# Windowed attention with q and k handled together: fewer, wider VectorE and GpSimd instructions, and alternating values matmuls

## The reference, cut to what matters

```python
h = shift_token(x)
q, k, v = jnp.split(h @ wqkv, 3, axis=-1)          # to 8 heads of 64
q = l2norm(q) * qs
k = l2norm(k) * ksc
q, k = rotary_xpos(q, k)                           # q*cos*scale + rotate_half(q)*sin*scale, k likewise with 1/scale
...
sim = jnp.einsum('bhwid,bhwjd->bhwij', bq * 8.0, look_around(bk))   # windows of 64, own and previous
attn = jax.nn.softmax(where(mask, -max, sim), axis=-1)
out = jnp.einsum('bhwij,bhwjd->bhwid', attn, look_around(bv))
x = x + out @ wo
...
x = x + (a * gelu(g)) @ w2 + b2                    # a, g from a layer norm and w1
```

## Time and profile before

| what | value |
|---|---|
| median of 3 runs | 2024.12 us (2023.77 to 2026.48) |
| the profiled execution, its own time | 2023.84 us |
| its span in the trace | 2022.0 us |
| PE, PEld busy | 1660.5 us (82%), 1363.3 us (67%) |
| DVE, ACT, POOL busy | 1419.8 us (70%), 1157.7 us (57%), 1091.1 us (54%) |
| mean granted TensorE clock | 0.937 |

### The profile page before, as it was taken

One profiled execution on the slowest core, in us unless ns is written; L12 is line 12 of the kernel. 1 busy time (PEld: TensorE's weight loads), 2 busy tenths in 40 slices (PEclk: granted clock), 3 DMA queues, 4 the chain that ended last, 5 costly groups with the idle time before them and its releaser, 6 DMA issues.

```text
span 2022.0 us, 48409 instructions
## 1 busy us (share of the span) xinstructions
PE 1660.5 (82%) x15864; PEld 1363.3 (67%) x15864; DVE 1419.8 (70%) x3769; ACT 1157.7 (57%) x3315; POOL 1091.1 (54%) x1090
## 2 busy tenths in 40 slices
PE   1898989888989899746756749989897889898984
PEld 1677878776878777525535537777776777777773
DVE  6686868676868687455655648868786768786873
ACT  1676757565757576412312227767675767576671
POOL 2774848464848485221231247757565657566650
PEclk9999999999999999978968979999998999999997
DMA  7231212122212121031010032111122221112113
GB/s 255 66 98 40 47 40 60 47 78 63 47 39 53 39 48 38 12 128 42 0 41 21 0 83 47 44 46 42 49 49 84 50 61 44 49 38 51 36 37 107
DMA packets 183672, 112.13 MB, mean 55 GB/s; under 512 B 86721, under 2 KB 164129, under 8 KB 182945
## 3 DMA queue, kind: packets, MB, share of 16 engines
q1 hardware_dynamic: 183456, 109.12, 20.4%
HBM read 43.41 MB, written 23.42 MB: 33 GB/s over the span
## 4 chain that ended last, share of the span: by engine, by line
PE 68%; DVE 11%; issue 6%; ACT 5%; SPq 3%; DMA 3%; POOL 2%; DVEq 0%; POOLq 0%; ACTq 0%
PE QK L345 12%; PE OB L690 10%; PE TT L578 7%; PE SC L619 6%; PE QK L578 5%; PE OB L645 5%; PE VB L345 4%; DVE o_n L977 4%; PE OB L578 4%; PE TT L345 3%; PE SC L601 2%; ACT probs L1098 2%; PE OB L745 2%; PE VB L745 2%; PE SC L782 2%
## 5 line engine op out<-in xcount | busy, mean ns | idle before, releaser
L1098 ACT ACTIVATE probs<-SC,shift,qgain 128x128 f32<-128x128 f32 x1024 | 457.4, 469 | 96.8 <-DVE shift L896 96.6
L1222 POOL TENSOR_TENSOR ve<-mv,epsilon 128x1 f32<-128x1 f32 x128 | 24.3, 190 | 529.1 <-DVE mv L940 529.1
L345 PE MATMUL QK<-w_qkv,hT 128*128 128x512 f32 x768 | 226.8, 433 | 19.9 <-DMA w_qkv<-qkv_d 10.5
L1098 ACT ACTIVATION_READ_ACCUMULATOR probs<-SC,shift,qgain 128x1 f32 x1024 | 220.0, 215 | 0.0
L1235 POOL TENSOR_TENSOR rnorm<-clip,mhalf 128x8 f32<-128x8 f32 x128 | 211.2, 1650 | 15.0 <-DVE clip L905 14.9
L578 PE MATMUL TT<-ident,probs 128*128 128x128 f32 x1280 | 194.4, 280 | 25.0 <-ACT probs L1098 18.4
L888 DVE TENSOR_REDUCE top<-SC 128x4 f32<-128x512 f32 x256 | 175.4, 685 | 56.0 <-PE SC L619 56.0
L1244 POOL TENSOR_TENSOR qgain<-clip,mhalf 128x8 f32<-128x8 f32 x128 | 209.4, 1636 | 0.0
L578 PEld LDWEIGHTS TT<-ident,probs 128*128 128x128 f32 x1280 | 156.9, 144 | 64.7 <-issue 20.8
L949 DVE TENSOR_TENSOR rope_c<-QK,rope 128x512 f32<-128x512 f32 x256 | 172.9, 676 | 35.9 <-PE QK L345 34.8
L954 DVE TENSOR_TENSOR rope_s<-QK,rope 128x256 f32<-128x256 f32 x512 | 190.3, 412 | 0.0
(11 more groups left out here) (136 smaller groups left out, 3908.6 us busy)
## 6 DMA issues: line engine op xcount, KB each, us to landing
v_prev<-v_own SPq DMA_DIRECT2D x256, 128.0 KB, 2.3
x_att<-stream SPq DMA_DIRECT2D x128, 64.0 KB, 2.1
h<-stream SPq DMA_DIRECT2D x256, 32.0 KB, 1.8
stream<-x_new SPq DMA_DIRECT2D x32, 256.0 KB
w_qkv<-qkv_d SPq DMA_DIRECT2D x3, 1536.0 KB, 6.6
h<-x_mid SPq DMA_DIRECT2D x128, 32.0 KB
h<-x_mid SPq DMA_DIRECT2D x128, 31.8 KB
rope<-rope_d SPq DMA_DIRECT2D x24, 128.0 KB, 3.2
```

The costliest lines, as they stand in the source:

```text
L345: last = mm(dst, fr(left(a)), fr(right(b)), start=(k == 0), stop=(k == 2))
L1098: last = nc.scalar.activation(probs[:, b, hd, :], SC[:, hd * P:hd * P + P], ACT.Exp, bias=shift[:, b, hd:hd + 1], scale=qgain[:, b, hd % 4 ...
```

## The change

DVE's rotation takes q and k in one instruction for the cosines and two for the sines, where there were two and four, and waits once, for both products. The maximum is one instruction over 8 heads and the shift one over 8 heads; both stand ahead of `o_n`. The clip is one instruction. The factor 8 on q, which was in the clip of q, is put into q's tables on the host. POOL adds q and k in one instruction into the new buffer `qk_r`, and scales the keys in it in place. ACT's first exponential waits for the single shift. The values product goes head by head, first and second window in turn.

```diff
-        q_r = sb("q_r", [P, 2, INNER])
-        k_a = sb("k_a", [P, INNER])
-        k_r = sb("k_r", [P, 2, INNER])
+        qk_r = sb("qk_r", [P, 2, 2 * INNER])
...
-                        for m, signal in ((0, s_q), (1, s_k)):
-                            product(mm, QK[:, m * 512:m * 512 + 512], lambda x: hT[:, b, x, :],
-                                    lambda x: w_qkv[:, x, m * 512:m * 512 + 512]).then_inc(signal, 1)
+                        for m in range(2):
+                            last = product(mm, QK[:, m * 512:m * 512 + 512], lambda x: hT[:, b, x, :],
+                                           lambda x: w_qkv[:, x, m * 512:m * 512 + 512])
+                        last.then_inc(s_k, 1)
...
-                        for w, v in ((0, v_prev), (1, v_own)):
-                            for hd in range(HEADS):
+                        for hd in range(HEADS):
+                            for w, v in ((0, v_prev), (1, v_own)):
...
-            def highest(t, half):
+            def highest(t):
 
                 dve.wait_ge(s_s, t.count())
-                v.tensor_reduce(top[:, t.i % 2, 4 * half:4 * half + 4],
-                                SC[:, half * 512:half * 512 + 512].rearrange("q (h k) -> q h k", h=4),
+                v.tensor_reduce(top[:, t.i % 2, :], SC[:, :].rearrange("q (h k) -> q h k", h=HEADS),
                                 AX, ALU.max).then_inc(s_mx, 1)
...
-                v.tensor_scalar(clip2[:, b, 8:16], norm2[:, b, 8:16], 1e-24, None, ALU.max).then_inc(s_cl, 1)
                 need(dve, s_qg, t.count(back=2))
-                v.tensor_scalar(clip2[:, b, 0:8], norm2[:, b, 0:8], 1e-24, QK_SCALE ** -2,
-                                ALU.max, ALU.mult).then_inc(s_cl, 1)
+                v.tensor_scalar(clip2[:, b, :], norm2[:, b, :], 1e-24, None, ALU.max).then_inc(s_cl, 1)
...
-                    need(dve, s_ka, t.count(back=1))
-                    for m, signal in ((0, s_q), (1, s_k)):
-                        dve.wait_ge(signal, t.count())
-                        src = qk(QK[:, :])[:, m]
-                        v.tensor_tensor(qk(rope_c[:])[:, m], src,
-                                        rope[:, i, m, 0:1, :].to_broadcast([P, HEADS, DH]), ALU.mult)
-                        sin = rope[:, i, m, 1:2, :]
-                        for half in range(2):
-                            a, o = 32 * half, 32 * (1 - half)
-                            last = v.tensor_tensor(qk(rope_s[:])[:, m, :, a:a + 32], src[:, :, o:o + 32],
-                                                   sin[:, :, a:a + 32].to_broadcast([P, HEADS, 32]), ALU.mult)
+                    dve.wait_ge(s_k, t.count())
+                    v.tensor_tensor(qk(rope_c[:]), qk(QK[:, :]),
+                                    rope[:, i, :, 0, :].unsqueeze(2).to_broadcast([P, 2, HEADS, DH]), ALU.mult)
+                    for half in range(2):
+                        a, o = 32 * half, 32 * (1 - half)
+                        last = v.tensor_tensor(qk(rope_s[:])[:, :, :, a:a + 32], qk(QK[:, :])[:, :, :, o:o + 32],
+                                               rope[:, i, :, 1, a:a + 32].unsqueeze(2).to_broadcast([P, 2, HEADS, 32]),
+                                               ALU.mult)
...
-                act.wait_ge(s_sh, t.count(unit=2) + (half - 1))
+                act.wait_ge(s_sh, t.count())
...
-                    g.tensor_tensor(q_r[:, b, :], rope_c[:, 0:512], rope_s[:, 0:512], ALU.add).then_inc(s_qr, 1)
-                    need(pool, s_kr, t.count(back=1))
-                    g.tensor_tensor(k_a[:], rope_c[:, 512:1024], rope_s[:, 512:1024], ALU.add).then_inc(s_ka, 1)
+                    g.tensor_tensor(qk_r[:, b, :], rope_c[:], rope_s[:], ALU.add).then_inc(s_qr, 1)
```

More of the change, by code:

```diff
@@ L164, in build @@
         clip2 = sb("clip2", [P, 2, 2 * HEADS])
-        rnorm = sb("rnorm", [P, 2, HEADS])
-        qgain = sb("qgain", [P, 2, HEADS])
+        rnorm = sb("rnorm", [P, 2, 2, HEADS])
         rope_c = sb("rope_c", [P, 2 * INNER])
         rope_s = sb("rope_s", [P, 2 * INNER])
-        q_r = sb("q_r", [P, 2, INNER])
-        k_a = sb("k_a", [P, INNER])
-        k_r = sb("k_r", [P, 2, INNER])
+        qk_r = sb("qk_r", [P, 2, 2 * INNER])
         qT = sb("qT", [P, 2, PAIRS, P])
@@ L333, in build @@
         w1_of = [(w_1[:, 0, :], w_1[:, 1, :]),
-                 tuple(buf[:].rearrange("p b n -> p (b n)")[:, 0:2 * HID] for buf in (q_r, k_r))]
-        y_T = q_r[:].rearrange("p b n -> p (b n)")
+                 tuple(qk_r[:, b, 0:2 * HID] for b in range(2))]
+        y_T = qk_r[:, 0, :]
         def fr(ap):
@@ L631, in f @@
                             pe.wait_ge(s_sq, t2.count())
-                        for m, src in ((1, k_r), (0, q_r)):
+                        for m in (1, 0):
                             for c in range(PAIRS):
-                                last = transpose(QK[:, m * 512 + c * P:m * 512 + c * P + P], src[:, b, c * P:c * P + P])
+                                at = m * 512 + c * P
+                                last = transpose(QK[:, at:at + P], qk_r[:, b, at:at + P])
                             last.then_inc(s_tqk, 1)
@@ L883, in _, with shifted @@
             last.then_inc(s_b1, 1)
-            def highest(t, half):
+            def highest(t):
                 dve.wait_ge(s_s, t.count())
-                v.tensor_reduce(top[:, t.i % 2, 4 * half:4 * half + 4],
-                                SC[:, half * 512:half * 512 + 512].rearrange("q (h k) -> q h k", h=4),
+                v.tensor_reduce(top[:, t.i % 2, :], SC[:, :].rearrange("q (h k) -> q h k", h=HEADS),
                                 AX, ALU.max).then_inc(s_mx, 1)
[L892 to L897, removed]
+            def shifted(t):
+                dve.wait_ge(s_mx, t.count())
+                v.scalar_tensor_tensor(out=shift[:, t.i % 2, :].rearrange("p (e c) -> p e c", e=2),
+                                       in0=top[:, t.i % 2, :].rearrange("p (e c) -> p e c", e=2), scalar=-1.0,
+                                       in1=rnorm[:, t.i % 2, 0, :].rearrange("p (c e) -> p e c", e=2),
+                                       op0=ALU.mult, op1=ALU.mult).then_inc(s_sh, 1)
             def clipped(t):
@@ L969, in step @@
                     dve.wait_ge(s_qg, t.count())
-                    highest(t, 0)
-                    shifted(t, 0)
+                    highest(t)
+                    shifted(t)
                 if t := tile(ATT):
@@ L1095, in exponentials @@
                 b = t.i % 2
-                act.wait_ge(s_sh, t.count(unit=2) + (half - 1))
+                act.wait_ge(s_sh, t.count())
                 for hd in range(4 * half, 4 * half + 4):
                     last = nc.scalar.activation(probs[:, b, hd, :], SC[:, hd * P:hd * P + P], ACT.Exp,
-                                                bias=shift[:, b, hd:hd + 1], scale=qgain[:, b, hd % 4 * 2 + half:hd % 4 * 2 + half + 1],
+                                                bias=shift[:, b, hd:hd + 1], scale=rnorm[:, b, 0, hd % 4 * 2 + half:hd % 4 * 2 + half + 1],
                                                 accum_out=psums[:, b, hd:hd + 1])
@@ L1233, in step @@
                     b = t.i % 2
-                    pool.wait_ge(s_cl, t.count(unit=2) - 1)
-                    g.tensor_tensor(rnorm[:, b, :], clip2[:, b, 8:16], mhalf[:, 0:8], ALU.pow).then_inc(s_rn, 1)
+                    pool.wait_ge(s_cl, t.count())
+                    g.tensor_tensor(rnorm[:, b, 1, :], clip2[:, b, 8:16], mhalf[:, 0:8], ALU.pow).then_inc(s_rn, 1)
                     pool.wait_ge(s_rn, t.count())
-                    pool.wait_ge(s_ka, t.count())
-                    need(pool, s_tqk, t.count(back=2, unit=2))
-                    g.tensor_tensor(k_r[:, b, :].rearrange("p (h d) -> p h d", h=HEADS),
-                                    k_a[:].rearrange("p (h d) -> p h d", h=HEADS),
-                                    rnorm[:, b, :].unsqueeze(2).to_broadcast([P, HEADS, DH]), ALU.mult).then_inc(s_kr, 1)
-                    pool.wait_ge(s_cl, t.count(unit=2))
+                    pool.wait_ge(s_qr, t.count())
+                    keys = qk_r[:, b, 512:1024].rearrange("p (h d) -> p h d", h=HEADS)
+                    g.tensor_tensor(keys, keys, rnorm[:, b, 1, :].unsqueeze(2).to_broadcast([P, HEADS, DH]),
+                                    ALU.mult).then_inc(s_kr, 1)
                     need(pool, s_p, t.count(back=2, unit=2))
-                    g.tensor_tensor(qgain[:, b, :], clip2[:, b, 0:8], mhalf[:, 0:8], ALU.pow).then_inc(s_qg, 1)
+                    g.tensor_tensor(rnorm[:, b, 0, :], clip2[:, b, 0:8], mhalf[:, 0:8], ALU.pow).then_inc(s_qg, 1)
                 if t := tile(QKV):
@@ L1265, in _ @@
                 vz = z[:, :, 2 * DIM:3 * DIM]
-                scaled = k_r[:].rearrange("p a (t c) -> p (a t) c", c=DIM)
+                scaled = qk_r[:, 1, :].rearrange("p (t c) -> p t c", c=DIM)
```

6 lines of the change are left out of this document (1 added, 5 removed).

## The result

The changed kernel takes **2104.38 us** (median of 4 runs, 2101.84 to 2106.4), against 2025.3 us for the kernel before on the same chip: a ratio of 1.0386, 95% interval 1.0365 to 1.0406. The forecast was 2099, in a range of 2040 to 2160.

What follows compares the result with a forecast made beforehand. The prediction took PE's and ScalarE's loops as about equally tight, with ScalarE's deciding after the change. Terms 48 + 11 + 7 + 9 = 75 us on 2023.84 gave 2099 us, with 80% in 2040 to 2160.

Steps and rivals of the forecast that it cites:

- Bound: Ordinary step of 9.54 us: PE's and ScalarE's loops about equally tight; what delays the first exponential delays S.
- Values product: PE's alternating windows take 1.1 us instead of 1.9, a gain of 0.8 us of PE time per step.
- Rival 2: PE's saving comes through: `o_n` decides, period 9.31, 2000 to 2010 us; together with the 1922 us case 6%.
- Rotation and `h2n`: VectorE's rotation starts at S + 1.80, `h2n` at S + 4.1, held by GpSimd's `k_r` to S + 4.6.
- rival 3: The two shifts cancel: `h2n` not held, rotation's wait costs less, period near 9.8, 2025 to 2060 us; 12%.
- Maximum and shift: VectorE's maximum takes 0.54 us more; `shift` starts at S + 5.95, 0.16 to 0.23 ahead of GpSimd's addition.
- Rival 1: `shift` loses the race to GpSimd's addition in ordinary steps too: period 12.7, about 2320 us; 10%.
- ScalarE's loop: First exponential at S + 6.23, then 4.02 us to the next S: period 10.25, +48 us over 75 intervals.
- Step behind a burst: First stack: addition first, `shift` held, `o_n` +1.85 us; second stack: free, 0.25 earlier; together +11 us.
- Bursts: Intervals with a burst: exponentials 0.8 later, partly won back by the norm no longer held, +0.5 x 14 = +7 us.
- the two burst terms: Intervals with a burst, +7 us, and steps directly behind a burst, +11 us.
- Rival 4: TensorE's clock falls to 1.2 GHz in some steps as PE idles before `o_n` and `oT`: above 2150 us; 6%.

Runs made afterwards that it cites:

- experiment 2: Changed kernel with the values product back in the old order, one window behind the other: 2105.39 us, 1.0394 against the kernel before.
- Experiment 1: Kernel before with only the values product changed, head by head with the two windows in turn: 1986.37 us, 0.9803.
- Experiment 3: Changed kernel with maximum and shift in two halves again, the exponentials waiting for their half: 2046.87 us, 1.0111 against the kernel before.
- experiment 6: Changed kernel with the rotation in six instructions again, q's three as soon as q's product is there: 2054.92 us, 1.0147 against the kernel before.
- experiment 12: Experiment 8 with maximum and shift over 8 heads at once ahead of `o_n`: 2051.33 us, 1.0124 against the kernel before.
- 8: Experiment 1 with `h2n` between the rotation of q and that of k, and the clips behind `mv`: 1977.61 us, 0.9765 against the kernel before.
- experiment 4: Changed kernel with `h2n` moved ahead of the rotation on VectorE: 2076.21 us, 1.0248 against the kernel before.
- experiment 9: Changed kernel with one tiny GpSimd instruction (128x1) added directly ahead of the merged addition: 2077.3 us, 1.0256 against the kernel before.
- 7: Changed kernel with maximum and shift in halves and `h2n` ahead of the rotation, both at once: 2103.61 us, 1.0386 against the kernel before.

## Why the prediction was right, point by point

- **Bound.** Right for the kernel after: the loop through `top`, `shift` and the exponentials decides, and experiment 2 shows that PE's earlier values product then earns nothing. Wrong in part for the kernel before: the two loops were not equally tight. PE's, through the values product and `o_n`, set the period, and ScalarE's had some 0.33 us of slack. Experiment 1, which relieves PE alone, shows it: the first exponential stays, and the time from it to the next S falls from 4.10 to 3.76 us. So "what delays the first exponential delays S" holds only from about 0.33 us of delay on.
- **Values product.** 1.1 predicted, 1.15 measured. Rival 2 (PE's saving comes through) did not happen. That its 9.31 is close to the 9.29 of experiment 1 is luck: there `o_n` starts at S + 5.43 and not S + 5.95.
- **Rotation and `h2n`.** S + 1.80 and S + 4.1 predicted, 1.77 and 4.11 measured; `h2n` held to S + 4.76 instead of 4.6. But "`k_r` runs at about S + 3.55" is not what the kernel before does. In the step of the earlier trace rows it starts at S + 4.07, with `mv` at S + 0.84:

  ```profile
  519.02 1.04 POOL L1239 TENSOR_TENSOR k_r<-k_a,rnorm 128x512 f32<-128x512 f32 x1
  ```

  In its median ordinary step `mv` is at S + 1.20 and `k_r` at S + 4.31. There `h2n` at S + 4.11 would have been 0.2 ahead of it and free, as in rival 3. In the changed kernel `mv` comes at S + 0.44 and the scaling at S + 3.63, and only so the two meet. Experiment 3, the changed kernel with the halves back, has `mv` at S + 0.96 or later in most ordinary steps and the scaling at S + 4.14 or later, so the earlier GpSimd comes from the single maximum and shift: no second shift stands ahead of `norm` and all that follows it. The prediction names no reason for its S + 3.55; the place was right, the reading of the kernel before was not.

  The Trainium skill, page "SBUF — State Buffer", section "Who interferes with whom", says that whoever issues first gets the shared ports; by that, the `h2n` of experiment 6, which starts 0.03 ahead of the scaling, should be free. By the starts in the trace this does not hold (1.15 us instead of 0.34), and the measurement decides. The trace tells of starts and not of issues, and its times on GpSimd are rough, so which of the two was issued first stays open. The prediction's own "the trace agrees" also passes over the exception that it names: `shift` is not stopped by `qgain`.
- **Maximum and shift.** S + 5.95 and a lead of 0.16 to 0.23 predicted, 5.99 and 0.24 measured. Rival 1 needed the race to turn in ordinary steps; it did not.
- **ScalarE's loop.** The mis-sized term of the ordinary step: "I take 4.02 (between 3.98 and 4.12)", because "Behind that `qT` PE can't start much sooner". From first exponential to next S it takes 3.77. In the step of the earlier trace rows `oT` ended at 523.17 and `qT` at 524.14, 0.35 ahead of S; PE's output product started only at 523.67, directly behind its transposes:

  ```profile
  523.24 0.60 PE L578 MATMUL TT<-ident,probs 128*128 128x128 f32 x4
  ...
  523.67 1.06 PE L645 MATMUL OB<-w_o,oT 128*128 128x128 f32 x8
  ```

  In the trace after it starts 0.05 behind `oT`, and S comes 0.10 behind `qT`: 0.25 of the 4.02 was PE's and not ScalarE's. The old order of the values product (experiment 2) has the same 3.77, so in the changed kernel PE's slack comes from the late `shift` and would be there without the alternation; experiment 1 has it from the alternation, without a late `shift`. 75 x 0.25 is 19 us too much; the first exponential, 0.04 later than forecast, and nine intervals of 10.15 to 10.36 give some 5 of it back.
- **Step behind a burst.** Right in mechanism, too small in number: "In the second stack ... free" failed. The lead forecast there was 0.21; the scaling began 1.39 ahead of `top` in the trace after instead of 1.02, since `mv` came earlier, at S + 0.55 instead of S + 0.92, and the addition won by 0.05. A lead of 0.2 us, built from rows of another schedule, was no basis for "free".
- **Bursts.** +0.5 each predicted, +1.0 measured: the mis-sized term is "+0.5 x 14". In the step with the burst `h2n` is held to S + 5.00 and the first exponential comes at S + 6.52, 1.1 later than the S + 5.42 of the earlier trace rows and not 0.8. In experiment 6, where `h2n` is free in this step and the exponential 0.57 earlier, the interval is 0.6 shorter; so a burst pays for the late exponentials one to one. That the sum came within 3 us of the measured one is partly luck: -13 in the ordinary steps against +13 in the two burst terms.
- **Clock.** Rival 4 did not happen; in ordinary steps (527 to 547 us of the trace) the granted clock was 1.00, the 2.4 GHz level. It did fall, before and after, behind the bursts, where PE idles for `o_n` and at the loop's end (0.86 and 0.83 in the mean of the 14 intervals), which the prediction had no term for.
- **The two parts of the cost.** In ordinary steps, by the means of the same 75 intervals, the merged maximum costs 0.47 us (experiment 12 against 8) and the held `h2n` 0.30 (experiment 4). Alternation gives 0.28 back from the old period: 9.60 - 0.28 - 0.06 (order of experiment 8) + 0.47 + 0.30 = 10.03, where 10.07 was measured. The held `h2n` is not the merged rotation's alone: experiment 6 takes that back, `h2n` comes at S + 3.61, and is held all the same, since the scaling starts at S + 3.64. Outside ordinary steps, the held shift behind bursts costs 27 us (experiment 9).

## What to carry to other kernels

Merging instructions saves their fixed cost (VectorE's busy time fell by 58 us here) and takes away the places where the consumer could start and where another engine could get in; ask of each merge who waited for its first half. When two engines share a port, list each short instruction's distance to the other's wide one, stage by stage: a forecast lead of under 0.2 us is a coin toss worth the whole length of the wide one. Holds don't add up, since one delay moves the instruction that would have caused the next; experiments 3, 4 and 7 gave -57, -28 and together -1.

## What the runs showed of the hardware

- Two thresholds for the hold, by the starts in the traces. Over all 14 kernels, `h2n` (128x128) was held to the end of GpSimd's wide instruction when it started up to 0.09 us ahead of it, and free from 0.11 on. `shift` (128x8 or 128x4) was free from a lead of 0.02, both free and held at 0.01, and held to the end when it started behind. `o_n`, which reads PSUM and one SBUF operand, was never held (0.68 to 0.69 us in all 1792, of which 196 start inside a wide one). GpSimd's power of 128x8, 1.64 us long, holds neither: 1410 shifts of 0.16 to 0.20 us lie wholly inside one.
- The records of the values product (two for each matmul) start 0.06 us apart when they are of one window. With the windows in turn they start in pairs, one record of each window within 0.01 us, and the pairs are 0.06 us apart: 1.15 us for all 32 records instead of 1.9.
- PE's idle time at the loop's end takes 2.8 to 4.0 us in 12 places of each trace (mean 3.62 before, 3.34 after). It overlaps little with PE's wait for `o_n` ahead of it: experiment 9 takes 2.13 us of that wait away, and the interval is 2.3 us shorter.
